# A fused transformer step on one core: pairwise row maxima in the second attention, stored key features in the first layer

## What is computed

```python
x = x + attn_a(layernorm(x))     # 16 heads of 64, random-feature attention, then an ELU feed-forward net
x = x + ffn(layernorm(x))        # 160 experts, 8 per token, and a shared expert
x = x + attn_b(layernorm(x))     # 16 heads of 8, causal softmax attention
x = x + ffn(layernorm(x))        # the same expert layer again

# attn_a, key side:  dash = (k * dn) @ proj.T ; diag = sum(k*k) * dn*dn / 2
#                    kf = ratio * (exp(dash - diag - max(dash)) + 1e-6)    the maximum is over all keys
# its feed-forward:  h = elu(out1 @ W1 + b1) ; h @ W2 + b2
# attn_b:            softmax(causal(q @ k.T) / sqrt(8)) @ v
```

## Time and profile before

| what | us |
|---|---|
| median of 3 runs (lowest to highest) | 2456.73 (2450.88 to 2458.65) |
| the profiled execution, its own time | 2462.02 |
| its span in the trace | 2459.9 |
| key_maximum | 0 to 83.3 |
| attn_a, batches 0 to 3 | 83.3 to 213.5, to 404, to 601, to 794 |
| ffn_a | 794 to 830 |
| first expert layer | 830 to 1132 |
| layer_b (its slots) | 1132 to 1952 (1200 to 1952) |
| second expert layer | 1952 to 2460 |

### The profile page before, as it was taken

One profiled execution on the slowest core, in us unless ns is written; L12 is line 12 of the kernel. 1 busy time (PEld: TensorE's weight loads), 2 busy tenths in 40 slices (PEclk: granted clock), 3 DMA queues, 4 the chain that ended last, 5 costly groups with the idle time before them and its releaser, 6 DMA issues. The chain is left out here.

```text
span 2459.9 us, 45628 instructions
## 1 busy us (share of the span) xinstructions
PE 1858.3 (76%) x15915; PEld 1074.0 (44%) x15915; DVE 1640.3 (67%) x4684; ACT 1106.3 (45%) x2069; POOL 1261.6 (51%) x1244
## 2 busy tenths in 40 slices
PE   8998888877888678782989988988898778784000
PEld 3556446445555556561334443434343346563000
DVE  8357577578568665385888888887888365375322
ACT  1363544545445446561357644544454546663000
POOL 0153146656657676675246530342153467577776
PEclk9999989989989879896689987898898979997555
DMA  9400000100100688783314221203121288785222
GB/s 370 174 1 5 1 1 24 35 16 18 35 22 31 249 294 263 240 280 118 78 52 115 60 65 39 63 31 89 29 84 51 104 295 271 250 274 180 61 60 56
DMA packets 134252, 275.69 MB, mean 112 GB/s; under 512 B 29644, under 2 KB 44620, under 8 KB 128124
## 3 DMA queue, kind: packets, MB, share of 16 engines
q1 hardware_dynamic: 101256, 205.60, 25.4%
q0 software_dynamic: 32768, 67.17, 9.3%
HBM read 146.34 MB, written 125.93 MB: 111 GB/s over the span
## 5 line engine op out<-in xcount | busy, mean ns | idle before, releaser
L1504 POOL DMA_INDIRECT slots_in<-g_xs,g_place x512 | 508.6, 993 | 298.8 <-ACT b_pT L2595 145.9
L2595 ACT ACTIVATE b_pT<-b_psE 128x512 f32<-128x512 f32 (+3 forms) x768 | 331.8, 492 | 374.4 <-PE b_psE L2496 206.7
L1531 POOL DMA_INDIRECT r_xs<-slots_out,g_place x336 | 328.3, 977 | 228.4 <-issue 86.2
L2347 DVE TENSOR_REDUCE b_peak<-b_psM 128x1 f32<-128x512 f32 (+3 forms) x768 | 387.9, 549 | 78.1 <-PE b_psM L2479 45.4
L2476 PE MATMUL b_psM<-b_stacks 72*128 72x512 bf16 (+3 forms) x768 | 260.1, 376 | 56.7 <-DVE b_peak L2347 24.7
L2492 PE MATMUL b_psE<-b_stacks 75*128 75x512 bf16 (+3 forms) x768 | 235.6, 361 | 14.7 <-ACT b_pT L2595 12.9
L1531 POOL DMA_INDIRECT g_xs<-slots_out,g_place x176 | 173.9, 988 | 93.4 <-issue 50.9
L2506 PE MATMUL b_psV<-b_pT,b_vb 128*32 128x512 f32 (+3 forms) x1536 | 180.4, 552 | 4.0 <-ACT b_ctxu L2602 3.7
L2476 PEld LDWEIGHTS b_psM<-b_stacks 72*128 72x128 bf16 x768 | 79.5, 105 | 224.9 <-DVE b_peak L2347 133.9
L2112 DVE COPY m_staged_w<-wgd 128x192 f32 x512 | 108.1, 281 | 86.2 <-PE m_psY L1817 75.2
L2112 DVE COPY n_staged_w<-wgd 128x192 f32 x512 | 106.1, 277 | 83.3 <-PE n_psY L1817 47.1
(11 more groups left out here) (664 smaller groups left out, 4068.3 us busy)
## 6 DMA issues: line engine op xcount, KB each, us to landing
wgd<-in_w_gdT SPq DMA_DIRECT2D x20, 1536.0 KB, 10.5
slots_in<-g_xs SPq DMA_DIRECT2D x26, 1024.0 KB
m_rows<-slots_in SPq DMA_DIRECT2D x104, 256.0 KB
slots_out<-m_y SPq DMA_DIRECT2D x104, 256.0 KB
n_rows<-slots_in SPq DMA_DIRECT2D x104, 256.0 KB
slots_out<-n_y SPq DMA_DIRECT2D x104, 256.0 KB
b_stacks<-q_parts SPq DMA_DIRECT2D x48, 192.0 KB
b_stacks<-k_parts SPq DMA_DIRECT2D x48, 192.0 KB
```

The costliest lines, as they stand in the source:

```text
L1504: self.nc.gpsimd.indirect_dma_start(self.G.slots_in[self.h], bass.IndirectOffsetOnAxis(self.G.place[:, TPH * self.h + t, k:k + 1], 0), sel ...
L1531: self.nc.gpsimd.indirect_dma_start(self.rows(i)[:, k, :], None, self.G.slots_out[t // TPH], bass.IndirectOffsetOnAxis(self.G.place[:, t, ...
L2347: nc.vector.reduce_max(to, taking()[:, 0:size], AX.X).then_inc(m_taken, 1)
L2595: nc.scalar.activation(pT[:, e % KEPT, h, q0:HALF], psE[:, j % BANKS, q0:HALF], ACT.Exp, scale=SCALE).then_inc(e_taken, 1)
```

## The change

**First layer.** `key_maximum` now makes each dash with tokens on partitions (the turned x is stationary, wkp streams), as the key phase did. ACT copies it from PSUM to one of four buffers in SBUF, DVE takes the maximum there, and SP stores it to DRAM. In the key phase SP loads it back into arg, two tiles deep; key_dash leaves PE, and DVE's argument works in place in SBUF. Values get two banks, and add_kv runs two tiles behind. The zero fills are spread: one for each four dashes, one for each key tile of batch 0, the rest at the end of that batch's SP program. The ELU's two parts are added on DVE, and PE multiplies the sum once.

**Second attention.** Stacks of 64 rows (the ninth product and so the last 8 rows are left out) of two heads lie on the two halves of the partitions, in a new buffer `halves`; they serve the maxima alone. Two matmuls of 64 rows, one of each head, go to two banks, and one DVE maximum takes both if the banks are neighbours. SP loads the halves with 12 DMAs for each two heads. `logits` and `probs` share memory with `parts`, and DVE waits for the store before it writes them.

```diff
@@ key_maximum, sync
-            for slots in G.slots_in:
-                fill = slots.rearrange("(n p j) d -> n p (j d)", n=ZERO_FILLS, p=P)
-                for n in range(ZERO_FILLS):
-                    sp.dma_start(fill[n], G.zeros[:]).then_inc(zero_fills, 16)
+            for n in range(TILES):
+                sp.wait_ge(copied, n + 1)
+                sp.dma_start(G.key_dash[n], dashes[:, n % KEPT_F, :]).then_inc(kept[n % KEPT_F], 16)
+                if n % 4 == 3:
+                    A.fill_zeros(sp, 1)
+            for k in kept:
+                sp.wait_ge(k, 16 * TILES // KEPT_F)
@@ key_maximum, tensor
-                        last = nc.tensor.matmul(psF[:, n % RING_F, u, :], wkp[:, c, :], G.xnT[:, b, u * HALF:(u + 1) * HALF], start=True, stop=True)
+                        last = nc.tensor.matmul(psF[:, n % RING_F, u, :], G.xnT[:, b, t * P:(t + 1) * P],
+                                                wkp[:, 4 * u:4 * u + 4, :].rearrange("p c m -> p (c m)"), start=True, stop=True)
@@ key_maximum, scalar
+            for n in range(TILES):
+                b, t = divmod(n, TPB)
+                act.wait_ge(feats, n + 1)
+                if n >= KEPT_F:
+                    act.wait_ge(kept[n % KEPT_F], 16 * (n // KEPT_F))
+                    act.wait_ge(taken, n - KEPT_F + 1)
+                nc.scalar.activation(dashes[:, n % KEPT_F, :], psF[:, n % RING_F, :, :].rearrange(both), ACT.Copy).then_inc(copied, 1)
@@ key_maximum, vector
-                    nc.vector.reduce_max(pmax[:, b, c:c + 1], psF[:, n % RING_F, :, :].rearrange(both), AX.X).then_inc(taken, 1)
+                    nc.vector.reduce_max(pmax[:, b, t:t + 1], dashes[:, n % KEPT_F, :], AX.X).then_inc(taken, 1)
@@ attn_a, vector
+                nc.vector.drain()
                 nc.vector.reduce_sum(shift[:], fold2[:, t % 2, :, :], AX.X).then_inc(k_diag, 1)
...
-                nc.vector.tensor_tensor(arg[:, t % 2, :].rearrange(heads, k=MF), dash, bc(shift[:], MF), ALU.subtract).then_inc(k_arg, 1)
+                dve.wait_ge(kd_landed[t % 2], 16 * (t // 2 + 1))
+                argument = arg[:, t % 2, :].rearrange(heads, k=MF)
+                nc.vector.tensor_tensor(argument, argument, bc(shift[:], MF), ALU.subtract).then_inc(k_arg, 1)
@@ attn_a, sync
+            for t in range(TPB):
+                if t >= 2:
+                    sp.wait_ge(k_exp, t - 1)
+                sp.dma_start(arg[:, t % 2, :], G.key_dash[TPB * b + t]).then_inc(kd_landed[t % 2], 16)
+                if b == 0:
+                    A.fill_zeros(sp, 1)
+                elif t == 1:
+                    routing_loads(sp, W, R)
             if b == 0:
+                A.fill_zeros(sp, HALVES * ZERO_FILLS)
                 sp.wait_ge(zero_fills, 16 * HALVES * ZERO_FILLS)
@@ attn_a, tensor
                 fill(t, 0)
+                key(t)
                 fill(t, 1)
-                key(t)
+                if t >= 2:
...
+                    add_kv(t - 2, range(HA // 2))
                 fill(t, 2)
+                if t >= 2:
+                    add_kv(t - 2, range(HA // 2, HA))
                 fill(t, 3)
-                key_dash(t)
+                values(t, 0)
                 fill(t, 4)
+                values(t, 1)
+                fill(t, 5)
@@ ffn_on_tensor and ffn_limits
-        for part, ready in ((B.high, B.up_taken), (B.low, B.low_ready)):
...
+        pe.wait_ge(B.elu_ready, FFC * u + c + 1)
+        for t in range(PER):
+            last = nc.tensor.matmul(B.psY[:, u, t * DM:(t + 1) * DM], B.low[u][:, c, t * P:(t + 1) * P], F.w2[:, c, :],
+                                    start=(c == 0 and t == 0), stop=(c == FFC - 1), skip_group_check=True)
...
+            dve.wait_ge(B.up_taken, FFC * u + c + 1)
+            nc.vector.scalar_tensor_tensor(B.low[u][:, c, :], B.low[u][:, c, :], 1.0, B.high[u][:, c, :],
+                                           ALU.min, ALU.add).then_inc(B.elu_ready, 1)
@@ layer_b
+    ROWS_M = 8 * WB
+    BLOCKS_M = ((1, 0, 3 * WB), (2, 3 * WB, 3 * WB), (0, 6 * WB, 2 * WB))
...
+                c, (first, second) = ring.next_two()
+                dve.wait_ge(m_done, c)
+                if second == first + 1:
+                    nc.vector.reduce_max(to, psM[:, first:second + 1, 0:size], AX.X).then_inc(m_taken, 2)
+                else:
+                    nc.vector.reduce_max(to[:, 0:1], psM[:, first, 0:size], AX.X)
+                    nc.vector.reduce_max(to[:, 1:2], psM[:, second, 0:size], AX.X).then_inc(m_taken, 2)
...
+                for i, bank in enumerate(banks):
+                    rows = slice(ROWS_M * i, ROWS_M * (i + 1))
+                    last = nc.tensor.matmul(psM[:, bank, 0:n], halves[rows, two, 0, qt * P:(qt + 1) * P],
+                                            halves[rows, two, 1, kh * HALF:kh * HALF + n], start=True, stop=not diagonal,
+                                            skip_group_check=diagonal)
                 if diagonal:
+                    for bank in banks:
+                        last = nc.tensor.matmul(psM[:, bank, n - P:n], ident_bf[:], mask_q[:], start=False, stop=True, skip_group_check=True)
+                last.then_inc(m_done, 2)
...
+            def load_halves(group, two):
...
+                if group:
+                    sp.wait_ge(m_done, maxima_end[group - 1, two])
...
+                for odd in range(2):
+                    head = g * HG + 2 * two + odd
+                    for i, at, count in BLOCKS_M:
+                        for n, (src, step) in enumerate(((G.q_parts, 0), (G.k_parts, P))):
+                            sp.dma_start(halves[ROWS_M * odd + at:ROWS_M * odd + at + count, two, n, :],
                                         src[i * step:i * step + 3 * P, cols].rearrange("(r h) n -> r h n", h=HB)[0:count, head, :]
                                         ).then_inc(halves_landed[two], 16)
@@ layer_b, sync, in the loop over the groups
+                    if b and not last and g == 1:
+                        store(b + 1)
+                    load_halves(b * GB + g + 2, 0)
                     if not (last and g == GB - 1):
                         peaks(b * GB + g + 1, (g + 1) % GB)
+                    load_halves(b * GB + g + 2, 1)
```

186 lines of the change are left out of this document (96 added, 90 removed).

## The result

After takes 2483.4 us (median of 4 runs, 2476.0 to 2500.0), before 2456.8 (4 runs): a ratio of 1.0106, 95% interval 1.0072 to 1.0139. The change makes the kernel slower by 1.1%. The forecast was 2409 us, its range 2383 to 2440.

A forecast was written before the change was run, and what follows sets the result against it. PE was taken to bound batch 0's key tiles, PE and DVE by turns later, with PE, DVE and ACT close in the slots. 2462.0 profiled - 41.5 (first layer) - 6 (second attention) = 2414.5; median 5.3 lower: 2409 us, range 2383 to 2440.

The forecast's parts named there:

- First stage, +1: Stage up to the key tiles: PE's dashes cover ACT's copies, PE and ACT now follow the DMA engines, +1 us.
- batch 0, -13: Key tiles of batch 0: 8 x 1.71 = 13.7 us of PE's key_dash go, tiles of 5.4 us, -13 us.
- Rival (c): First layer: DMA engines hold it, costing 10 us in the first stage, 5 in batch 0's tiles; 2424 us, chance 0.1.
- Batches 1 to 3, -6.5 each for key_dash: Key tiles of batches 1 to 3: only the PE-bound stretch gives, three tiles x 1.71 and about 1.5 more.
- rival (b): Key tiles: DVE's routing covers them, batches 1 to 3 give only the ELU; -22 us, 2429 us, chance 0.13.
- the last section of the forecast: Signs of right or wrong; one wrong sign: DVE without a POOL wait in middle tiles while blocks keep their length.
- ELU, -2.5 a block: Feed-forward ELU, four batches: of 7.1 us of PE saved, DVE sees 2.5 each, between -1 and -7.
- Start of the attention, 0: Start of second attention: twelve issues, 5 us, replace the six PE waits for, 512 KB land no later; 0 us.
- Rival (e): Second attention: halves land late, twelve issues, 5 us, behind stack loads, 2 us a slot; 2439 us, chance 0.07.
- Slots, -6: Second attention's 16 slots: PE gains nothing, 0.4 of DVE's 1.4 us a slot counts; -6 us, between -25 and +58.
- rival (a): Second attention's pairs: halves do not run side by side, only switches are paid; +58 us, 2473 us, chance 0.1.
- Rival (d): Second attention: pairs pay in full, DVE and PE give 2 us a slot in 15 slots; -30, 2385 us, chance 0.1.

The follow-up runs named there:

- The last experiment: After's first layer with before's second attention, routing's first six products moved behind key(3) in PE's and ACT's programs: 0.9848 of before.
- the runs with single banks: After's first layer, old 72-row stacks, each maximum with its own bank and reduction, heads in turn, two to a PE program place: 1.0014 and 1.0019 of before.

## Why the forecast failed

- *First stage, +1, and batch 0, -13*: measured -0.3 and -15.2. Right, with its mechanism: tiles of 5.4 us and DMA at 413 GB/s. Rival (c) is false.
- *Batches 1 to 3, -6.5 each for key_dash*: the first step that failed. The sum took "three tiles x 1.71" off a stretch in which PE was busy 24.4 of 26 us. A busy PE was not what set the pace: with less on it, it ran ahead into its own waits (6.8 us for the argument, 3.0 and 3.8 for routing) and stood in front of key(3). The tiles stayed the same in sum (78.3 us for 78.8 of the ELU alone). It is rival (b), given 0.13: -22 for the first layer where the profile has -24.8, and DVE's wait for POOL did not vanish, as the rival and the last section of the forecast supposed, but moved behind the 20 us tile. The last experiment shows that PE's order, and not only DVE's work, held it: 12 us came back by a change of order.
- *ELU, -2.5 a block*: its own run has -10.8 us between the medians for -10, but not by this mechanism, so the agreement is luck as far as the traces tell. The front of the block of batch 1 gives 6.4 us where the sum had 2.5, the rest of it takes 8.3 back, the three blocks lie within the scatter of before (579.7 us for 575.8 to 581.5), and ffn_a gives 0.1 to 2.2.
- *Start of the attention, 0*: failed. The sentence "twelve issues, 5 us, replace the six for which PE waits" counted the first group's halves. The second group's 24 issues were placed behind 24 loads of stacks, and PE wants them before slot 0: +15.1, of which 3.0 are the expert layer's tail and 12.1 lie in `layer_b`; 10 to 13 us go when the loads are put in the order in which PE waits for them. Rival (e), "the halves land late", had the mechanism and looked for it in the slots, where the runs show nothing (762.0 for 762.7 us).
- *Slots, -6*: failed, and most. The prices were right (0.09 to 0.10 us for a change of height, 0.07 to 0.08 for a merged reduction, matmuls on row halves side by side), so rival (a) is false though its 2473 us lies nearest. What the sum left out is not a price of an instruction but two waits. The first has no term in it at all: two maxima now stand at one place of PE's program, with the scores behind them. The second is the sentence "PE now waits for two banks at a time", with no number behind it: 7.7 us in the first group's maxima, of which the halves return 4.5. Of 28 us, 12 to 18 come with the twos alone (the runs with single banks; up to 4 of it are the order), 4 to 5 more with the halves and two banks, which nearly cancel, and up to 10 are not assigned (above). Rival (d), the pairs pay in full, is false: 142 us less in the records of PE and its weight queue leave 16 to 20 us against the same pairs at full height on the slower chips, and that is less than the pairs cost.
- *The expert layers*: -7.8 and +3.2 with no cause in the change. The first one takes between 272 and 290 us in the profiles on the faster chips and the second between 504 and 514, with the same code: it is scatter, and the profiles' distance of 13.6 us instead of 26.6 is partly that.
- The Trainium skill's page "TensorEngine Tiling (Array Packing)", section Tiling Modes, says that a change of mode drains TensorE; by that rule, the trace agrees (0.09 to 0.10 us each way). The Trainium skill's same page, Overview, gives a speedup of up to two for contractions of 64 or less. For a pair's streams the trace agrees (two of 512 columns end within 0.39 us, the length of one record). For the stage it does not: 66 us more of idle time in the weight queue and 20 us more of its waits for DVE stand against 104 us saved on PE.

## What to carry to other kernels

Taking work off the engine that looks busiest gains only where nothing else is due next: read, tile by tile, what ended the waits just before the stretch that looks full, and then move the order of the in-order engine too, which here was worth 12 us in three blocks where the removal alone was worth about 5. Two small jobs made one (two banks, two reductions, two matmuls) make an in-order engine wait in larger pieces, and in a ring of four banks jobs of two leave the two engines working in turn; compare first with the same pieces on the old data, which is a small edit, and read a stretch where nothing else runs. And a new transfer goes into the queue by when its reader wants it, not beside its kin.
